# Three of sixteen softmax units: minima subtracted on GpSimd, one 512-column exponential, sums on VectorE

## The reference

```python
x = x + tanh(g_xattn) * attention(layernorm(x), ctx, ctx, mask)   # then W_o, b_o
x = x + tanh(g_ffn)   * top1_moe(layernorm(x))                    # 16 experts, gelu, capacity 160
# attention: 16 heads of 16 features, windows of 64 tokens; a query window sees its own
# and the preceding window (128 keys), causal; softmax over these 128 keys
sim  = where(mask, q k^T / 4, -max);  attn = softmax(sim);  out = attn v
```

## Time and profile before

| what | value |
|---|---|
| median of 3 runs | 326.13 us (325.70 to 327.31) |
| the profiled execution | 324.84 us, of which the span is 323.1 us |
| mean granted TensorE clock | 0.993 of full |
| busy share of the span | PE 93%, DVE 61%, ACT 54%, POOL 51% |
| exp instructions (L697) | 256, of 128 x 128 elements |

### The profile page before, as it was taken

The page is one execution under the profiler, slowest core; times in us unless marked ns, Lnnn a source line. Parts: engine busy times, 40 slices in busy tenths (PEclk is TensorE's granted clock), DMA queues, the critical chain, the costliest instruction groups (busy, mean ns, idle before and its releaser), DMA issues.

```text
span 323.1 us, 8432 instructions
## 1 busy us (share of the span) xinstructions
PE 300.2 (93%) x2760; PEld 245.6 (76%) x2760; DVE 196.2 (61%) x953; ACT 175.1 (54%) x662; POOL 164.5 (51%) x193
## 2 busy tenths in 40 slices
PE   7869879999999999999899899999999999999994
PEld 3438646887758866777778679898998989898974
DVE  2888898898989879899984223432415161515133
ACT  3379999999999999999743011111120202111110
POOL 6469647789769974979855022131313121121322
PEclk9997999999999999999999999999999999999999
DMA  7821199017512280230233589697989898998900
GB/s 219 281 90 25 40 380 330 10 26 242 184 67 92 62 298 3 100 79 19 83 122 149 123 235 370 179 377 200 372 246 353 270 333 267 294 324 247 367 22 13
DMA packets 48470, 60.54 MB, mean 187 GB/s; under 512 B 14712, under 2 KB 41360, under 8 KB 46384
## 3 DMA queue, kind: packets, MB, share of 16 engines
q1 hardware_dynamic: 45328, 53.29, 51.9%
q0 software_dynamic: 2560, 6.25, 5.3%
q10 hardware_dynamic: 544, 0.52, 0.5%
HBM read 44.60 MB, written 14.19 MB: 182 GB/s over the span
## 4 chain that ended last, share of the span: by engine, by line
PE 58%; ACT 26%; DVE 8%; issue 5%; DMA 1%; POOL 1%; SPq 0%; DVEq 0%; POOLq 0%; ACTq 0%
PE bank L1728 22%; ACT probs L697 18%; PE bank L1741 16%; PE bank L1766 5%; PE bank L1391 3%; ACT probsT L710 3%; DVE probs L927 3%; ACT q_par L671 2%; PE bank L1402 2%; PE bank L1504 2%; PE bank L1444 1%; DMA x_all<-in_x_dram 1%; PE bank L1466 1%; PE bank L1751 1%; PE bank L1413 1%
## 5 line engine op out<-in xcount | busy, mean ns | idle before, releaser
L697 ACT ACTIVATE probs<-probs,low 128x128 f32<-128x128 f32 x256 | 99.3, 405 | 2.2 <-DVE low L927 2.2
L518 POOL TENSOR_TENSOR probs<-probs,r_total 128x512 f32<-128x512 f32 x64 | 66.3, 1047 | 19.1 <-DVE r_total L936 18.7
L1728 PE MATMUL bank<-xdT,w 128*128 128x160 f32 x512 | 72.4, 299 | 2.1 <-issue 1.6
L1728 PEld LDWEIGHTS bank<-xdT,w 128*128 128x128 f32 x512 | 71.0, 190 | 4.0 <-issue 3.3
L927 DVE CUSTOM_DVE_ANT_0 probs<-bank,mask_now 128x128 f32<-128x128 f32 x256 | 57.2, 284 | 8.0 <-PE bank L1432 7.6
L697 ACT ACTIVATION_READ_ACCUMULATOR probs<-probs,low 128x1 f32 x256 | 52.5, 205 | 0.0
L857 ACT ACTIVATE w_raw<-bank 128x480 f32<-128x480 f32 (+1 forms) x24 | 12.6, 526 | 61.0 <-PE bank L1728 39.1
L622 POOL DMA_INDIRECT out_dram<-base,place x16 | 14.0, 876 | 59.9 <-DVE base L1294 38.4
L631 POOL DMA_INDIRECT out_dram<-base,place x16 | 15.7, 980 | 53.2 <-DVE place L1287 42.1
L857 ACT ACTIVATE x_all<-bank 128x480 f32<-128x480 f32 (+1 forms) x24 | 12.6, 526 | 53.8 <-PE bank L1728 35.2
L1444 PE MATMUL bank<-ident,probs 128*128 128x128 f32 x256 | 36.2, 278 | 2.2 <-DVE probsT L946 1.8
(11 more groups left out here) (142 smaller groups left out, 485.1 us busy)
## 6 DMA issues: line engine op xcount, KB each, us to landing
w<-in_L_ffn_w_dram SPq DMA_DIRECT2D x32, 1024.0 KB
expert_queue<-empty_row SPq DMA_DIRECT2D x1, 5140.0 KB, 19.0
q_blocks<-expert_queue SPq DMA_DIRECT2D x64, 40.0 KB
base<-expert_queue SPq DMA_DIRECT2D x16, 129.0 KB
ctx_rows<-in_ctx_dram SPq DMA_DIRECT2D x4, 512.0 KB, 9.6
out_dram<-rows SPq DMA_DIRECT2D x4, 512.0 KB, 6.3
x_all<-in_x_dram SPq DMA_DIRECT2D x3, 512.0 KB, 7.3
v_shift<-v SPq DMA_DIRECT2D x12, 128.0 KB, 2.3
```

Of the source, the lines that this page charges most:

```text
L518: pool.tensor_tensor(probs[:, i % NP_], probs[:, i % NP_], r_total[:, i % NP_].unsqueeze(2).to_broadcast([P, PAIRS, 2 * WINDOW]), ALU.mult ...
L697: last = act.activation(probs[:, i % NP_, j], probs[:, i % NP_, j], ACT.Exp, scale=-1.0, bias=low[:, i % NP_, j:j + 1], accum_out=total[:, ...
L1728: last = pe.matmul(ps_hidden[m][:, c * CAP:(c + 1) * CAP], w1_sb[i % 2][:, k, f * P:(f + 1) * P], xdT[i % 2][:, k], start=(k == 0), stop=( ...
```

## The change

In units 11, 12 and 13 of each batch, twelve of 64 units in all, a new POOL instruction `lower_wide` computes low - p over 512 columns in place. ACT waits for it and takes one exponential of 512 columns without accumulating. DVE sums the unit's four rows of 128 with one reduction, waits for its own result, and then takes the reciprocal as before. The POOL instructions stand behind x1_norm of tile 3, behind norm 10 and behind norm 11.

```diff
+        lowered_wide, totals_ready = sem("lowered_wide"), sem("totals_ready")
...
+        WIDE = (11, 12, 13)
...
+            def lower_wide(n, i):
+                pool.wait_ge(scores_taken, value(n, UNITS, i + 1))
+                pool.tensor_tensor(probs[:, i % NP_], low[:, i % NP_].unsqueeze(2).to_broadcast([P, PAIRS, 2 * WINDOW]),
+                                   probs[:, i % NP_], ALU.subtract).then_inc(lowered_wide, 1)
...
                 x1_norm(b - 1, 3)
+                lower_wide(b, 11)
                 norm(b, 10)
+                lower_wide(b, 12)
                 norm(b, 11)
+                lower_wide(b, 13)
                 mask_of(b + 2)
...
             x1_norm(LAST - 1, 3)
+            lower_wide(LAST, 11)
             norm(LAST, 10)
+            lower_wide(LAST, 12)
             norm(LAST, 11)
+            lower_wide(LAST, 13)
             norm(LAST, 12)
...
             def exp(n, i):
                 if not 0 <= n < B:
                     return
+                if i in WIDE:
+                    act.wait_ge(lowered_wide, value(n, len(WIDE), WIDE.index(i) + 1))
+                    act.activation(probs[:, i % NP_], probs[:, i % NP_], ACT.Exp).then_inc(exp_done, 1)
+                    return
...
                 dve.wait_ge(exp_done, value(n, UNITS, i + 1))
+                if i in WIDE:
+                    dve.tensor_reduce(total[:, i % NP_], probs[:, i % NP_], AX.X, ALU.add).then_inc(totals_ready, 1)
+                    dve.wait_ge(totals_ready, value(n, len(WIDE), WIDE.index(i) + 1))
                 dve.reciprocal(r_total[:, i % NP_], total[:, i % NP_]).then_inc(r_total_ready, 1)
```

## The result

The changed kernel takes 344.62 us (median of 4 runs, 344.28 to 344.80) and the kernel before 325.91; the ratio is 1.0577, 95% interval 1.054 to 1.0614. It is slower by 18.7 us. The direction was forecast, but not the size: 338.5 was forecast, 12.6 above the kernel before, and the range ended at 343. An execution more than 1.5% longer than the shortest of its kernel counts as slow; it stays in a median and is left out of a ratio.

What follows compares the result with a forecast made beforehand. Attention was taken as bound by queue order, with POOL late and ACT fullest, its delay passing to the PE-bound experts. Batch delays of 1.5, 3.2, 4.1 and 4.2 us gave 13.0, forecast 338.5 us, range 332 to 343.

Steps and rivals of the forecast that it cites:

- the sum: Attention's four batches: delays of 1.5, 3.2, 4.1 and 4.2 us, added to 13.0 us.
- rival of 10%: PE idle in batches 1, 2 and last: TensorE's clock falls, 1 to 4 us more, 340 to 343; 10%.
- choose beside POOL: DVE's choose slowed while POOL works: 0.2 us added in batch 1, 0.8 in batch 2; 0.7 taken back in last.
- queue walk: Attention's units 11 to 13: ACT waits for POOL's late minima; batches 1.5, 3.2, 4.1 and 4.2 us late.
- prices: Per wide unit: lower_wide 1.03 us, exponential 0.48, ACT giving back 1.06; reduction 0.6, with its wait 0.65 on DVE.
- No difference: POOL's minima ready when ACT comes: DVE's 2.6 us less ACT's 2.5, about 0, some 326 us; 5%.
- Faster: ACT bounds and POOL's lateness isn't real: ACT's 12.7 us less DVE's 7.8 leaves -4.9, so 321; 4%.
- slack rival: Uncounted waits on PE or DMA where the next batch begins give back 3 to 6 us, 332 to 336; 15%.

## Why the prediction was wrong

**The step that failed.** It is the sum, which left TensorE's clock out and so put it at nothing. The prediction saw that PE would stand "some 4.5 us before chunk 1" (it was 4.98) and that the clock had fallen to 0.50 behind an idle 2.69, and then filed it as a rival of 10%, worth 1 to 4 us for the whole kernel. A fall after a shorter idle time stood in its own rows, and the last batch was to stand longer, so it belonged in the sum with more than 10%. In the profiled last batch it was 4.5 us (+8.9 as it came, +4.4 with the clock held), two thirds of the 6.6 us by which the four stretches exceed the sum (19.6 against 13.0). By medians the held clock gave back 1.7 to 2.7 us in all, and where the clock came back after some 3 us the same batch cost +5.1: the term is real, but its size changes from execution to execution. Nor was the fall certain. In the run with minima early PE has the same idle time in batch 0 and the clock does not fall:

```profile
23.78 1.17 PE L1453 MATMUL bank<-kT,q_par 32*128 32x128 f32 x32 [2.69 <-ACT q_par L685]
```

```profile
26.00:28.00 2.00, 1.75 (x13) 1.36 (x11) 2.00 (x21) 2.00 (x12) 2.00 (x3) 1.00 0.00 0
```

**The second term mis-sized** is choose beside POOL. I read the earlier trace rows as a wait for one POOL instruction and added 0.2 us in batch 1. There the three instructions are, in the changed kernel and then in the kernel before,

```profile
85.50 1.10 DVE L1044 SCALAR_TENSOR_TENSOR marks<-lowered,countdown 128x64 f32<-128x64 f32 x1
...
86.52 0.63 DVE L1048 TENSOR_TENSOR scaled<-lowered,rstd 128x64 f32<-128x64 f32 x1
...
87.32 1.07 DVE L1053 TENSOR_TENSOR onehot<-marks,best 128x64 bf16<-128x64 f32 x1
```

```profile
81.86 0.51 DVE L1023 SCALAR_TENSOR_TENSOR marks<-lowered,countdown 128x64 f32<-128x64 f32 x1
...
82.29 0.21 DVE L1027 TENSOR_TENSOR scaled<-lowered,rstd 128x64 f32<-128x64 f32 x1
...
82.67 0.94 DVE L1032 TENSOR_TENSOR onehot<-marks,best 128x64 bf16<-128x64 f32 x1
```

2.80 us together and 1.66 before: +1.1. That is most of what batch 1 exceeds its forecast by (4.5 against 3.2). In batch 2 the three grew by 0.5, not 0.8, and in the last batch they shrank by 1.3, not 0.7. So the term's total, +0.3, came out as forecast, by luck: no single batch did.

SBUF — State Buffer of the Trainium skill, in its section Who interferes with whom, has the shared port pair go to whichever of the two starts first, for that whole instruction. The traces agree that one is held while the other runs, but in the run with POOL's work alone `marks` was held past three instruction ends, 3.59 us, and so the measurement goes beyond the page.

**The queue walk was right, batch 1 aside.** POOL without a gap, the waits of unit 11 (3.19, 3.80 and 5.70 us), batch 2 (4.4 against 4.1) and, at a steady clock, the last batch (4.4 against 4.2). In batch 0 it was 1.8 against 1.5, of which 0.35 lies ahead of the first wide unit. Batch 2 owes some of its closeness to chance, since choose beside POOL grew 0.3 less than was added for it, and its clock was low for some 3 us, whose cost no run shows.

**The prices.** `lower_wide` 1.033 us as taken; the wide exponential 0.54 from start to start (82.56 to 83.10), not 0.48, so ACT gives back 1.0 a unit and 12.0 in all, not 12.7; the reduction 0.68, not 0.6. For the reduction the prediction had an estimate of 0.6 to 0.7 from VectorE: DVE Perf Modes of the Trainium skill, with which the row agrees. The sums cost 5.2 us by a run of their own; the walk had six of them, 3.9 us, on the path.

**The rivals.** "No difference" assumed that ACT's 2.5 us would pay for DVE's sums once POOL is in time: the run without minima costs +5.3 instead, and ACT's saving pays nothing. "Faster" falls by ACT's waits of 19.2 us, and ACT's saving alone would not have gained anything. The slack rival falls: no stretch was less late than forecast.

**The account.** The loss is 18.7 us. Taking the minima early leaves 9.8: 8.9 us are the late queue, with PE's idle time and what it does to the clock. Leaving out POOL's work as well leaves 5.3: 4.5 are that work and what came with it in that run. The last 5.3 are the sums.

## What to carry to other kernels

An instruction handed to an engine with idle time is not free: ask what stands ahead of it in that engine's queue at the moment when the consumer is ready, and what its neighbours lose to a run without gaps. Walk the order with start times, then ask of each stall whether it leaves TensorE idle for as long as a stall after which the same trace shows a low clock; if it does, the slower matmuls belong in the sum. And price a saving on the busiest engine by what follows it: here 12 us off ScalarE were worth nothing (330.77 against 330.68), though which engine took over the pace was not settled.

## What the hardware showed that I had not expected

- A VectorE instruction of 64 columns with two SBUF inputs, 0.23 us long where GpSimd rests, was held beside back-to-back GpSimd instructions for 3.59 and 4.67 us, to the end of their run. With the same work behind it it took 0.63 and 0.68, the second in the middle of such a run: either can happen.
- What the clock does after one and the same stall differs from execution to execution. After 4.98 us of idle TensorE it was low for 11 us in one and some 3 in another, of two kernels with the same code there; after 2.69 us it fell to 0.50 in one and stayed at 1.00 in another. The executions of the run with GpSimd's work alone lay 6.7 us apart, with mean granted clocks of 0.973 to 0.995.
- Sixteen matmuls on idle data (3.63 us) in the stall kept the clock at 1.00 and gave back 4.5 us of the batch between two profiled executions, 1.7 to 2.7 us by the medians.
